# One of a unit's sixteen turns of maxima folded in the loop: a relu by ScalarE and one pass of VectorE in place of two reductions

## The chip, the cores and the metric

The kernel runs on one core of a Trainium2 chip. The metric is the device time of the whole program in microseconds, taken as the median of several executions. The profiled execution is one more of them, seen from inside.

## What is computed

The input is x, 2 sequences of 1024 tokens of 128 features. The reference is one layer of a transformer with the norm behind each part: sixteen-head attention with heads of 8 features, a residual and a layer norm, then a feed-forward part with weights that are small whole numbers, a residual and a second norm.

```python
scores = einsum('bhqd,bhkd->bhqk', q, k) * (1 / sqrt(16))
attn = softmax(scores, axis=-1)
out = einsum('bhqk,bhkd->bhqd', attn, v)
x = layernorm(x + out @ wo.T + bo)
h = silu(x @ w1.T * s1) * (x @ w2.T * s2)
h = gelu(h @ h1.T * s); h = gelu(h @ h2.T * s)
x = layernorm(x + h @ w3.T * s3)
```

The change touches only the maximum of each row of scores, which the softmax subtracts.

## The kernel before, in words

**Units.** Attention is done in 16 units (U_ALL). A unit is one of two sequences, a group of four heads (HG) of the sixteen, and one half of the queries (512, C). Units 2g and 2g+1 share group g of keys and queries, which lie in slot g % 2 of the tiles kx and qx. The scores are computed twice. The first time they have queries on the partitions and keys along a row, only to find each row's largest score. The second time they have keys on the partitions, so that their exponentials can be fed to the products with v. The maxima enter this second pass as additional rows of qx, which is why they have to be there before a unit's first score tile.

**Turns and halves.** A unit has 16 turns (TURNS): four heads by four blocks of 128 queries. Turn t has two halves, m = 2t and 2t+1, one for each 512 of the 1024 keys. For each half TensorE does one matmul of 128x512 into one of four PSUM banks (turn_half, L1265), and VectorE takes its largest value by a TENSOR_REDUCE (turn_half of VectorE, L976). TensorE waits before half m until the reduction of half m-4 has emptied the bank. When a unit's 16 turns are done, larger (L986) takes the smaller of the two negated maxima. POOL then splits them into three bfloat16 parts (split_max, L828 to L834), TensorE turns them (L1314), ScalarE copies them out (copy_max, L671), and SP sends them by two DMAs into qx (load_max, L405). The score tile that begins a unit waits for these DMAs (mrow_in).

**The folded turns of the prologue.** Turns 5 to 26 are done in another way, because ScalarE is free there. With d = k1 - k0, the difference of the two key halves of one head, max(q.k0, q.k1) = q.k0 + relu(q.d). TensorE computes q.d and q.k0 (fold_apart, fold_first), ScalarE takes the relu of q.d out of PSUM into SBUF (copy_over, L684), and VectorE adds q.k0 and takes the maximum in one pass (turn_folded, L966). That pass is two instructions in the profile: the custom operation and the read of its accumulator. The difference of keys is made for group 0 only, from proj, split in two parts, sent through d_dram, and loaded as kd.

**The loop.** From turn 27 (WHOLE) on, halves, scores and products are interleaved by groups g, written out in the program: three halves (turn_halves), three score tiles (scores_of, L1327) in pairs with them, and then 384 columns of products of each of four heads (product, L1343). Maxima are 54 halves ahead of the scores: half m stands beside score tile m - 54. A score tile needs a PSUM bank of three (bank_plan). Its bank comes free when ScalarE has taken the exponential of an earlier tile (exp, L663), as a rule that of three tiles before. At the end of a unit ScalarE copies the unit's products out (copy_unit, L676), and the bank plan moves the score tiles to the bank that this empties. After turn 255 the rest of the units goes on without maxima. VectorE's and SP's parts are hardware loops over four units (Fori, ITERS); those of TensorE and ScalarE are written out.

**SP's queue.** Before its loop SP issues, in the order of the program: unit 0's maxima, loads of group 1, stores of batch 1's keys and queries to DRAM, the biases and wo, five small vectors, and it waits for the stores. Then the loop begins with the maxima of unit 1.

Of the kernel before, what the change touches and what calls it, by code (L numbers as in the profile page):

```python
# [36 lines left out]
H, DH = 16, 8  # L37
# [30 lines left out]
FOLD = 5  # L68
TURN_AFTER, COPY_AFTER = 5, 6
# [133 lines left out]

def apart_bank(t):
    return FOLD_BANKS[(t - FOLD) % len(FOLD_BANKS)]

# [5 lines left out]
def build(nc, xT, wqT, wkT, wvT, woT, bq, bk, bv, bo, late,  # L212
          w1s, w2s, h1s, h2s, w3s, k_dram, q_dram, d_dram, den_dram, out):
    with ExitStack() as ctx:
# [17 lines left out]
        kd_part = [w_high[:, PAIR + j, :] for j in range(HALVES)]  # L232
        w_low = nc.alloc_sbuf_tensor_at("w_low", [P, SLICES, HID], F32, offset=LATE_AT)
# [18 lines left out]
        def over_sb(t):  # L252
            return attn[:, U_ALL - 4 + t % 4, :]

# [64 lines left out]
        kd_in = sem("kd_in")  # L319
        over = sem("over")  # L320
# [92 lines left out]
        def _(sp):  # L413
# [50 lines left out]

            def load_max(i, w):

                sp.wait_ge(max_copied, i * PER + w + 1)
                for r in range(2):
                    spread_max(sp, r, w)
# [13 lines left out]
            for r in range(2):  # L483
                for i in range(HALVES):
                    at = r * GROUP + i * HALVES * DH
                    sp.dma_start(kd[at:at + HALVES * DH].bitcast(F32),
                                 d_dram[r * PAIR:(r + 1) * PAIR].rearrange("h d j t -> (d j) h t"))\
                      .then_inc(kd_in, 16)
# [15 lines left out]
            load_q(1, 1, 1)  # L504
            sp.wait_ge(split_late, 2)
# [16 lines left out]

            with sp.Fori(0, ITERS - 1) as i:
# [4 lines left out]
                for slot in range(2):  # L528
                    base, g = i * (STEPS * HG) + slot * 2 * KT * HG, i * 2 + slot + 2
                    sp.wait_ge(scores, base + KT * HG)  # L530
                    load_q(g, slot, 0)
                    sp.wait_ge(scores, base + KT * HG * 3 // 2)
                    load_k(g, slot, 0, C, rows_in[slot][0])
                    load_max(i, 2 * slot + 2)
                    sp.wait_ge(scores, base + KT * HG * 2)
                    load_k(g, slot, C, L, rows_late[slot])
                    load_q(g, slot, 1)
                    if slot == 0:
                        load_max(i, 3)
# [68 lines left out]
        def _(act):  # L608
# [38 lines left out]
            act.dma_start(d_dram[:, :, 0].rearrange("h d t -> (h d) t"), kd_part[0][0:HG * DH, :])\  # L647
               .then_inc(apart_out, 16)
            act.wait_ge(apart_low, 1)
            act.dma_start(d_dram[:, :, 1].rearrange("h d t -> (h d) t"), kd_part[1][0:HG * DH, :])\  # L650
# [34 lines left out]

            for t in range(FOLD, WHOLE):
                copy_over(t)
                if t == TURNS + COPY_AFTER:
                    copy_max(0)
            for g in range(-RUN_BEFORE, GROUPS_ALL):  # L690
# [4 lines left out]
                else:  # L695
                    late_unit = None
                for n in scores_of(g):
                    exp(n)
# [83 lines left out]
        def _(pool):  # L782
# [67 lines left out]
            split_max(None, 0)  # L850
            pool.wait_ge(v_ready, NC_)
# [63 lines left out]
        def _(dve):  # L915
# [55 lines left out]
            def turn_half(i, m):  # L971

                dve.wait_ge(max_scores, i * (2 * PER * TURNS) + m + 1)
                t = m // 2
                h, q = head_of(t % (PER * TURNS) + PER * TURNS)
                nc.vector.tensor_reduce(negmax[:, t // TURNS % 2, m % 2, h * QT + q:h * QT + q + 1],  # L976
# [225 lines left out]
        def _(pe):  # L1202
# [41 lines left out]
            def turn_half(m):  # L1244
# [4 lines left out]
                if 2 * WHOLE <= m < 2 * WHOLE + 4:  # L1249

                    pe.wait_ge(max_taken, 2 * (m - WHOLE - 3))
                elif m >= 4:

                    pe.wait_ge(max_taken, m - 3)
# [3 lines left out]
                if part == 0:  # L1258
# [3 lines left out]
                    elif t % TURNS == 0:  # L1262

                        pe.wait_ge(rows_in[slot][qc], (t // (PER * TURNS) + 1) * LOAD_INC[qc])
                nc.tensor.matmul(ps[:, half_bank(m), :],  # L1265
                                       qx[at, slot, qc, h, q * P:(q + 1) * P],
                                       kx[at, slot, h, part * C:(part + 1) * C], start=True, stop=True)\
# [337 lines left out]
```

## Time and profile before

| | us |
|---|---|
| median of 3 runs | 445.57 (444.91 to 445.75) |
| the profiled execution's own time | 443.76 |
| its span, first to last instruction | 442.0 |
| TensorE busy | 427.3 |
| VectorE busy | 386.2 |
| ScalarE busy | 367.7 |
| POOL busy | 90.4 |

PE is TensorE's matmuls, PEld its loads of weights, DVE is VectorE, ACT ScalarE, and SPq the issue of DMAs by SP. A row of the groups by line has the line, the engine, the operation, out<-in by the program's names, partitions x elements and the count; then the busy time in us and the mean ns of one; then the idle time of the engine ahead of them, and what ended it. Where instructions overlap at their ends, busy time divided by count is the time from one to the next. A row of the timeline has the start in us, the length in us, the engine, the line, the operation and the count, and in brackets the idle time of the engine before it and who ended that. In the chain a row is start, length and what ran.

### The profile page before, as it was taken

How to read it: one execution, taken by the hardware profiler on the slowest of the kernel's cores; microseconds unless marked ns; L12 is line 12 of the kernel's file. 1: busy time of each engine (PE TensorE's matmuls, PEld its weight loads, DVE VectorE, ACT ScalarE, POOL GpSimd, SP SyncE). 2: the span in 40 equal slices, each digit the busy share in tenths (PEclk: the TensorE clock that was granted, in tenths of full speed). 3: DMA queues.
4: the chain of work that ended last, by engine and by line, in shares of the span. 5: the costliest groups of instructions: out<-in, count | busy, mean ns of one | idle time of the engine just before them, and what ended most of it. 6: DMA issues, size and time to landing. Idle time of an engine off the chain costs nothing.

```text
span 442.0 us, 9804 instructions
## 1 busy us (share of the span) xinstructions
PE 427.3 (97%) x3484; PEld 226.0 (51%) x3484; DVE 386.2 (87%) x721; ACT 367.7 (83%) x694; POOL 90.4 (20%) x142
## 2 busy tenths in 40 slices
PE   8999999999999999999999999999899899999993
PEld 3544444444444444444444443544333488877882
DVE  6699999999999999999999999999874576657636
ACT  4487989988998999989899899999899885678762
POOL 9820000100000010000001002372311363046103
PEclk9998999999999999999999999999999999999998
DMA  5566741100130111013011011121021000000101
GB/s 157 170 208 135 264 146 33 45 27 28 47 122 25 46 31 28 27 47 122 25 50 29 26 27 49 15 42 53 12 43 44 13 8 1 1 2 2 47 1 47
DMA packets 17117, 24.88 MB, mean 56 GB/s; under 512 B 5169, under 2 KB 9009, under 8 KB 16689
## 3 DMA queue, kind: packets, MB, share of 16 engines
q1 hardware_dynamic: 16464, 23.68, 19.0%
q10 hardware_dynamic: 608, 0.59, 0.5%
q8 instruction: 30, 0.49, 0.5%
q14 instruction: 15, 0.11, 0.1%
HBM read 15.08 MB, written 7.60 MB: 51 GB/s over the span
## 4 chain that ended last, share of the span: by engine, by line
PE 81%; DVE 10%; ACT 5%; issue 2%; DMA 0%; POOL 0%; SPq 0%; POOLq 0%; DVEq 0%; ACTq 0%
PE ps L1343 26%; PE ps L1265 20%; PE ps L1450 15%; PE ps L1327 11%; DVE negmax L976 9%; ACT arena L663 2%; PE ps L1206 2%; PE ps L1217 2%; PE ps L1396 1%; PE ps L1293 1%; PE ps L1237 1%; ACT v_pad L721 1%; PE ps L1281 1%; DMA qx<-mT 0%; PE ps L1406 0%
## 5 line engine op out<-in xcount | busy, mean ns | idle before, releaser
L976 DVE TENSOR_REDUCE negmax<-ps 128x1 f32<-128x512 f32 x458 | 275.5, 677 | 1.1 <-PE ps L1265 1.0
L663 ACT ACTIVATE arena<-ps 128x512 f32<-128x512 f32 x360 | 190.1, 605 | 18.5 <-PE ps L1327 13.6
L1327 PE MATMUL ps<-qx,kx 64*128 64x512 f32 x512 | 171.0, 453 | 1.3 <-DVE negmax L976 0.9
L1265 PE MATMUL ps<-kx,qx 61*128 61x512 f32 x468 | 160.6, 442 | 0.7 <-ACT arena L684 0.6
L1265 PEld LDWEIGHTS ps<-kx,qx 61*128 61x128 f32 x468 | 75.5, 185 | 89.2 <-DVE negmax L976 79.3
L1343 PE MATMUL ps<-arena,v_pad 128*32 128x256 f32 (+3 forms) x1328 | 105.2, 408 | 2.9 <-ACT arena L663 2.9
L663 ACT ACTIVATE hf<-ps 128x512 f32<-128x512 f32 x152 | 83.1, 603 | 9.3 <-PE ps L1327 8.3
L1327 PEld LDWEIGHTS ps<-qx,kx 64*128 64x128 f32 x512 | 79.2, 185 | 18.0 <-ACT arena L663 11.0
L1450 PE MATMUL ps<-hid,w_high 128*128 128x512 f32 (+1 forms) x296 | 68.2, 387 | 0.8 <-issue 0.4
L1450 PEld LDWEIGHTS ps<-hid,w_high 128*128 128x128 f32 x296 | 54.2, 188 | 12.3 <-issue 0.8
L1343 PEld LDWEIGHTS ps<-arena,v_pad 128*32 128x32 f32 x1328 | 28.6, 108 | 37.2 <-issue 31.1
L1343 PE MATMUL ps<-hf,v_pad 128*32 128x128 f32 (+1 forms) x600 | 47.5, 388 | 0.0
L1107 DVE TENSOR_TENSOR hid<-hf,hid 128x512 fp32r<-128x512 f32 x32 | 23.0, 726 | 19.6 <-ACT hid L737 19.6
L828 POOL TENSOR_TENSOR mpart<-negmin,zeros 128x16 bf16<-128x16 f32 x15 | 3.3, 221 | 144.4 <-DVE negmin L986 144.4
L887 POOL TENSOR_TENSOR hid<-hf,hid 128x512 fp32r<-128x512 f32 x16 | 20.6, 1320 | 32.6 <-ACT hid L727 32.6
L1343 PEld LDWEIGHTS ps<-hf,v_pad 128*32 128x32 f32 x600 | 15.7, 109 | 16.1 <-issue 9.8
L808 POOL COPY v_pad<-v_sb 128x256 f32 (+1 forms) x8 | 3.1, 398 | 87.2 <-PE ps L1343 87.1
L736 ACT ACTIVATE hf<-ps,h2s_sb 128x512 f32<-128x512 f32 x16 | 11.0, 687 | 10.7 <-PE ps L1450 10.7
L736 ACT ACTIVATE hf<-ps,h1s_sb 128x512 f32<-128x512 f32 x16 | 11.0, 686 | 8.7 <-PE ps L1450 8.7
L1089 DVE SCALAR_TENSOR_TENSOR hf<-ps,w2s_sb,v_pad 128x512 f32<-128x512 f32 x16 | 11.5, 740 | 7.3 <-ACT v_pad L721 7.3
L856 POOL TENSOR_TENSOR w_low<-late_sb,w_high 128x512 fp32r<-128x512 f32 x11 | 14.1, 1282 | 16.4 <-ACT w_high L710 16.4
L1450 PE MATMUL ps<-prt,w_high 128*128 128x512 f32 x64 | 16.4, 403 | 0.6 <-DVE hf L1089 0.6
(98 smaller groups left out, 313.4 us busy)
## 6 DMA issues: line engine op xcount, KB each, us to landing
qx<-parts_q SPq DMA_DIRECT2D x60, 64.0 KB, 2.1
late_sb<-in_late SPq DMA_DIRECT2D x3, 1280.0 KB, 5.6
kx<-parts_k SPq DMA_DIRECT2D x56, 64.0 KB, 2.1
parts_q<-prt SPq DMA_DIRECT2D x3, 512.0 KB, 5.2
parts_q<-arena SPq DMA_DIRECT2D x3, 512.0 KB, 6.8
xT_sb<-in_xT SPq DMA_DIRECT2D x4, 256.0 KB, 4.2
xT_sb<-arena SPq DMA_DIRECT2D x28, 32.0 KB
prt<-den SPq DMA_DIRECT2D x7, 128.0 KB
```

The source lines that it names most:

```text
L663: nc.scalar.activation(probs(n // HG)[:, heads(n), :], ps[:, PLAN["score", n][0], :], ACT.Exp, scale=SCALE).then_inc(exp_done, 1)
L736: nc.scalar.activation(hf[:, m % RING, :], bank, ACT.Gelu, scale=scale).then_inc(gelu_done, 1)
L856: nc.gpsimd.tensor_tensor(half(w_low[:, n, :]), w_sb[:, n, :], w_high[:, n, :], ALU.subtract).then_inc(w_left, 1)
L887: nc.gpsimd.tensor_tensor(half(dst[:, 1, m, :]), hf[:, m % RING, :], dst[:, 0, m, :], ALU.subtract).then_inc(gate_ready, 1)
L976: nc.vector.tensor_reduce(negmax[:, t // TURNS % 2, m % 2, h * QT + q:h * QT + q + 1], ps[:, MAX_BANK + m % 4, :], AX.X, ALU.max, negate=T ...
L1089: return nc.vector.scalar_tensor_tensor(out=out, in0=ps[:, gate_bank(c, m) + 1, :], scalar=s_sb["w2s"][:, m:m + 1], in1=gate[:, m % 2, :], ...
L1107: nc.vector.tensor_tensor(half(dst[:, 1, m, :]), hf[:, m % RING, :], dst[:, 0, m, :], ALU.subtract).then_inc(gelu_ready, 1)
L1206: nc.tensor.matmul(ps[:, bank, 0:cols], nonzero[:, 0, 0:P], nonzero[:, 0, 0:cols], start=True, stop=True)
L1265: nc.tensor.matmul(ps[:, half_bank(m), :], qx[at, slot, qc, h, q * P:(q + 1) * P], kx[at, slot, h, part * C:(part + 1) * C], start=True, s ...
L1327: nc.tensor.matmul(ps[:, bank, :], kx[at, slot, h % PAIR, kt * P:(kt + 1) * P], qx[at, slot, qc, h % PAIR, :], start=True, stop=True)\
L1343: ins = nc.tensor.matmul(ps[32 * n:32 * n + 32, PLAN["pv", w][0], c0:c1], v_pad[:, w // QC % 2, kt, n, :], probs(k)[:, n, c0:c1], start=(k ...
L1450: return nc.tensor.matmul(dsts[n], half(stationary), half(moving), start=start, stop=stop)
```

## The change

In the loop, one turn of each unit is folded too: turn t with t % 16 = 12, from 28 to 236, which is 14 turns. For it

- TensorE computes q.d in the place of half 2t and q.k0 in the place of half 2t+1. The half that uses the bank of q.d next waits for the relu (over) and not for a reduction.
- ScalarE does the relu of q.d (copy_over_one) ahead of the exp of the score tile that stands beside half 2t.
- VectorE skips half 2t, and at half 2t+1 does one pass of the kind of turn_folded.

The differences of keys are needed for one head of each group (FOLD_HEAD). Those of batch 0 come from kd_part of the prologue. Those of batch 1 are made by POOL in three more passes over 128x512. SP stores both to d_dram and loads each group's head into kd_one: for group 1 ahead of the loop, for the others within it. Two stores for batch 0 stand before those of batch 1's keys. Two for batch 1, a wait for the landing of all four, and the load for group 1 stand right before the loop.

```diff
 FOLD = 5
+FOLD_AT, FOLD_END, FOLD_HEAD = 12, 240, 1
 TURN_AFTER, COPY_AFTER = 5, 6
...
+def folded(t):
+    return t % TURNS == FOLD_AT and WHOLE <= t < FOLD_END
+def folds_to(t):
+    return WHOLE - FOLD + (t - FOLD_AT) // TURNS
 def apart_bank(t):
...
         kd_part = [w_high[:, PAIR + j, :] for j in range(HALVES)]
+        kd_late = [w_high[:, PAIR + 3 + j, :] for j in range(HALVES)]
+        kd_one = w_high[:, PAIR + 5:PAIR + 7, :].bitcast(F32R)
         w_low = nc.alloc_sbuf_tensor_at("w_low", [P, SLICES, HID], F32, offset=LATE_AT)
...
             return attn[:, U_ALL - 4 + t % 4, :]
+        kd_both = attn[:, 3, :]
+        def over_one(t):
+            return attn[:, U_ALL - 2 + t // TURNS % 2, :]
...
         kd_in = sem("kd_in")
+        late_apart = sem("late_apart")
+        late_apart_out = sem("late_apart_out")
+        one_in = [sem(f"one_in{n}") for n in range(2)]
         over = sem("over")
...
+            def store_apart(b, g0, parts):
+                for j in range(HALVES):
+                    sp.dma_start(d_dram[b * NG + g0:(b + 1) * NG, :, :, j].rearrange("g h d t -> (g h d) t"),
+                                 parts[j][g0 * HG * DH:, :]).then_inc(late_apart_out, 16)
+            def load_one(g, slot):
+                for i in range(HALVES):
+                    sp.dma_start(kd_one[i * HALVES * DH:(i + 1) * HALVES * DH, slot, :].bitcast(F32),
+                                 d_dram[bass.ds(g, 1), FOLD_HEAD].rearrange("o d j t -> (o d j) t"))\
+                      .then_inc(one_in[slot], 16)
             def load_max(i, w):
...
                     sp.dma_start(kd[at:at + HALVES * DH].bitcast(F32),
-                                 d_dram[r * PAIR:(r + 1) * PAIR].rearrange("h d j t -> (d j) h t"))\
+                                 d_dram[0, r * PAIR:(r + 1) * PAIR].rearrange("h d j t -> (d j) h t"))\
                       .then_inc(kd_in, 16)
...
             load_q(1, 1, 1)
+            store_apart(0, 1, kd_part)
             sp.wait_ge(split_late, 2)
...
+            sp.wait_ge(late_apart, 3)
+            store_apart(1, 0, kd_late)
+            sp.wait_ge(late_apart_out, 2 * STORE_INC)
+            load_one(1, 1)
             with sp.Fori(0, ITERS - 1) as i:
...
                     load_q(g, slot, 0)
+                    load_one(g, slot)
                     sp.wait_ge(scores, base + KT * HG * 3 // 2)
...
             act.wait_ge(apart_high, 1)
-            act.dma_start(d_dram[:, :, 0].rearrange("h d t -> (h d) t"), kd_part[0][0:HG * DH, :])\
+            act.dma_start(d_dram[0, :, :, 0].rearrange("h d t -> (h d) t"), kd_part[0][0:HG * DH, :])\
                .then_inc(apart_out, 16)
             act.wait_ge(apart_low, 1)
-            act.dma_start(d_dram[:, :, 1].rearrange("h d t -> (h d) t"), kd_part[1][0:HG * DH, :])\
+            act.dma_start(d_dram[0, :, :, 1].rearrange("h d t -> (h d) t"), kd_part[1][0:HG * DH, :])\
                .then_inc(apart_out, 16)
...
                 nc.scalar.activation(over_sb(t), ps[:, apart_bank(t), :], ACT.Relu).then_inc(over, 1)
+            def copy_over_one(t):
+                act.wait_ge(max_scores, 2 * t + 1)
+                act.wait_ge(max_taken, 2 * (t - 4))
+                nc.scalar.activation(over_one(t), ps[:, half_bank(2 * t), :], ACT.Relu).then_inc(over, 1)
...
                     late_unit = None
+                ones_at = [m for m in turn_halves(g) if folded(m // 2) and m % 2 == 0]
                 for n in scores_of(g):
+                    if ones_at and n == scores_of(g)[ones_at[0] - turn_halves(g)[0]]:
+                        copy_over_one(ones_at[0] // 2)
                     exp(n)
...
             split_max(None, 0)
+            pool.wait_ge(max_split, 1)
+            for r in range(2):
+                nc.gpsimd.memset(kd_one[ROWS:GROUP, r].bitcast(F32), 0.0).then_inc(kd_set, 1)
+                pool.wait_ge(kd_set, r + 3)
+            pool.wait_ge(max_taken, 2 * WHOLE)
+            nc.gpsimd.tensor_tensor(kd_both, proj[:, 1, :], proj[:, 0, :], ALU.subtract).then_inc(late_apart, 1)
+            pool.wait_ge(late_apart, 1)
+            nc.gpsimd.tensor_copy(kd_late[0].bitcast(F32R), kd_both).then_inc(late_apart, 1)
+            pool.wait_ge(late_apart, 2)
+            nc.gpsimd.tensor_tensor(kd_late[1].bitcast(F32R), kd_both, kd_late[0], ALU.subtract).then_inc(late_apart, 1)
+            pool.wait_ge(late_apart, 3)
             pool.wait_ge(v_ready, NC_)
...
-                dve.wait_ge(max_scores, i * (2 * PER * TURNS) + m + 1)
                 t = m // 2
                 h, q = head_of(t % (PER * TURNS) + PER * TURNS)
+                one = folded(t) and not (isinstance(i, int) and not folded(i * PER * TURNS + t))
+                if one and m % 2 == 0:
+                    return
+                dve.wait_ge(max_scores, i * (2 * PER * TURNS) + m + 1)
+                if one:
+                    dve.wait_ge(over, i * PER + folds_to(t))
+                    nc.vector.tensor_tensor_reduce(over_one(t), ps[:, MAX_BANK + m % 4, :], over_one(t),
+                                                   -1.0, 3.0e38, ALU.add, ALU.min,
+                                                   negmax[:, t // TURNS % 2, 0, h * QT + q:h * QT + q + 1])\
+                      .then_inc(max_taken, 2)
+                    return
                 nc.vector.tensor_reduce(negmax[:, t // TURNS % 2, m % 2, h * QT + q:h * QT + q + 1],
...
                     pe.wait_ge(max_taken, 2 * (m - WHOLE - 3))
+                elif folded((m - 4) // 2) and m % 2 == 0:
+                    pe.wait_ge(over, folds_to((m - 4) // 2))
                 elif m >= 4:
...
                         pe.wait_ge(rows_in[slot][qc], (t // (PER * TURNS) + 1) * LOAD_INC[qc])
+                keys = kx[at, slot, h, part * C:(part + 1) * C]
+                if folded(t):
+                    g = t // (QC * TURNS)
+                    if part == 1:
+                        keys = kx[at, slot, h, 0:C]
+                    elif g == 0:
+                        keys = kd[at, h, :]
+                    else:
+                        pe.wait_ge(one_in[slot], (g + 1) // 2 * STORE_INC)
+                        pe.wait_ge(kd_set, 4)
+                        keys = kd_one[at, slot, :]
                 nc.tensor.matmul(ps[:, half_bank(m), :],
                                        qx[at, slot, qc, h, q * P:(q + 1) * P],
-                                       kx[at, slot, h, part * C:(part + 1) * C], start=True, stop=True)\
+                                       keys, start=True, stop=True)\
                   .then_inc(max_scores, 1)
...
     q_dram = nc.dram_tensor("parts_q", (HALVES, QC, G_ALL, HG, DH, HALVES, C), F32, kind="Internal").ap()
-    d_dram = nc.dram_tensor("parts_d", (HG, DH, HALVES, C), F32, kind="Internal").ap()
+    d_dram = nc.dram_tensor("parts_d", (G_ALL, HG, DH, HALVES, C), F32, kind="Internal").ap()
     den_dram = nc.dram_tensor("den", (B, HG, NG, L), F32, kind="Internal").ap()
```

## Rows read from the trace of the kernel before

**Rows 1.** The page's first part: busy time and share of the span.
```profile
PE 427.3 (97%) x3484; PEld 226.0 (51%) x3484; DVE 386.2 (87%) x721; ACT 367.7 (83%) x694; POOL 90.4 (20%) x142
```

**Rows 2.** Groups by line, VectorE: busy us, mean ns, idle us before them.
```profile
L976 DVE TENSOR_REDUCE negmax<-ps 128x1 f32<-128x512 f32 x458 | 275.5, 677 | 1.1 <-PE ps L1265 1.0
...
L966 DVE CUSTOM_DVE_ANT_0 arena<-ps,arena 128x512 f32<-128x512 f32 x22 | 13.5, 687 | 0.2 <-ACT arena L684 0.2
...
L966 DVE DVE_READ_ACCUMULATOR2_ANT negmax<- 128x1 f32 x22 | 1.8, 84 | 0.0
```

**Rows 3.** The chain of waits in time order (start, us), 170 to 200.
```profile
175.48 0.79 PE ps L1343 x16
...
177.59 0.78 PE ps L1343 x8
...
179.28 0.78 PE ps L1343 x8
...
191.71 0.78 PE ps L1343 x8
...
193.50 0.78 PE ps L1343 x8
```

**Rows 4.** Timeline at a unit's boundary, 171.5 to 181.
```profile
173.24 1.58 ACT L663 ACTIVATE hf<-ps 128x512 f32<-128x512 f32 x3 [0.29 <-PE ps L1327]
...
174.98 0.50 PE L1327 MATMUL ps<-qx,kx 64*128 64x512 f32 x1
...
176.42 0.62 ACT L676 ACTIVATE arena<-ps 128x512 f32<-128x512 f32 x1
...
178.30 0.49 PE L1265 MATMUL ps<-kx,qx 61*128 61x512 f32 x1
...
179.62 0.16 DVE L986 TENSOR_TENSOR negmin<-negmax 128x16 f32<-128x16 f32 x1
```

**Rows 5.** Timeline at another unit's boundary, 150 to 162.
```profile
157.85 0.85 PE L1343 MATMUL ps<-arena,v_pad 128*32 128x384 f32 x8 [0.40 <-ACT arena L663]
```

**Rows 6.** Timeline of SP, 20 to 75.
```profile
52.03 0.43 SPq L518 DMA_DIRECT2D h1s_sb<-in_h1s  x1
52.50 0.43 SPq L518 DMA_DIRECT2D h2s_sb<-in_h2s  x1
53.24 1.59 SPq L405 DMA_DIRECT2D qx<-mT  x2
```

**Rows 7.** Timeline of ScalarE, 48 to 49.5.
```profile
48.54 0.30 ACT L671 ACTIVATE mT<-ps 128x128 f32<-128x128 bf16 x1
```

**Rows 8.** Timeline of all engines, 53 to 63.
```profile
52.72 10.89 DVE L976 TENSOR_REDUCE negmax<-ps 128x1 f32<-128x512 f32 x18
...
56.39 0.18 PEld L1327 LDWEIGHTS ps<-qx,kx 64*128 64x128 f32 x1 [0.36 <-issue]
```

**Rows 9.** DMA issues by line: size and median us from issue to landing.
```profile
parts_k<-arena SPq DMA_DIRECT2D x1, 512.0 KB, 4.4
parts_k<-prt SPq DMA_DIRECT2D x1, 384.0 KB, 3.2
...
parts_k<-prt SPq DMA_DIRECT2D x1, 128.0 KB, 2.0
```

**Rows 10.** Groups by line, POOL.
```profile
L845 POOL TENSOR_TENSOR arena<-late_sb,prt 128x512 f32<-128x512 f32 x4 | 5.0, 1268 | 1.2 <-ACT prt L657 1.2
```

**Rows 11.** Busy time by stretch (PE, PEld, DVE, ACT, POOL), granted clock, DMA.
```profile
39.50:41.00 1.50, 1.50 (x7) 1.28 (x6) 1.50 (x3) 1.50 (x5) 0.00 (x0) 0.50 1.00 127
41.00:43.00 2.00, 2.00 (x12) 0.62 (x10) 2.00 (x4) 1.56 (x4) 0.00 (x0) 0.53 1.12 195
43.00:45.00 2.00, 2.00 (x28) 1.06 (x26) 1.37 (x5) 1.31 (x3) 0.00 (x0) 1.00 1.02 362
```

**Rows 12.** Timeline of TensorE, 31 to 44.
```profile
40.25 1.05 PE L1265 MATMUL ps<-kx,qx 61*128 61x512 f32 x2
...
43.12 0.49 PE L1265 MATMUL ps<-kx,qx 61*128 61x512 f32 x1
```

## The prediction

> **What bounds the kernel now.** I first read the page's busy shares: TensorE 97%, VectorE 87%, ScalarE 83% [rows 1]. They make TensorE look like the bound. The groups by line say otherwise: 458 maxima of a half (L976) cost 275.5 us of VectorE, so 0.60 us each back to back, and the engine idled only 1.1 us before all of them [rows 2]. From about 37 to 315 us VectorE never rests. The chain of waits then gives TensorE's pace. A group of the order (three key halves for maxima, three score tiles, 384 columns of products) starts every 1.79 us when VectorE sets it (3 x 0.60), and every 1.69 us right after a delay, when TensorE is catching up: 177.59 to 179.28. Once per unit, where ScalarE copies the unit out, a group takes 2.11 us: 175.48 to 177.59 [rows 3]. So TensorE's own time is close behind. Per unit (32 halves, 10.67 groups) VectorE needs 32 x 0.60 = 19.2 us. TensorE alone needs 10.67 x 1.69 = 18.0, plus 0.42 at that boundary, plus some 0.2 to 0.3 for the turn of the maxima: 18.7.
>
> **What a folded turn saves.** Turns 28, 44, ... 236 are folded: 14. Each loses two reductions, 1.20 us, and gets one pass as in the prologue: 13.5 / 22 = 0.61 us, its accumulator read of 0.08 beside the next pass (0.70 if it isn't) [rows 2]. VectorE is asked for 0.59 us less each, 8.3 us in all. The two matmuls stay. ScalarE gets a relu of 0.60 us, 0.49 in a row of others (three exps take 1.58, so 0.49 from start to start) [rows 2, 4].
>
> **What is kept of it.** I walk one fold through the rows. In the group at 173 us it falls on the second and third pair, so the relu stands between the exps of 173.24 and 173.73. The third exp then starts at 174.69 and not at 174.21, and ends at 175.29. The score tiles have three PSUM banks, so the third tile of the next group, now at 174.98, waits for that exp: 175.34, 0.36 later. ScalarE reaches the copy-out of the unit at 176.7, not 176.42, and the third tile after it waits for the copied bank, so the group of 178.30 starts near 178.6 [rows 4]. Its first half can be reduced from 179.13. Before, VectorE took it at 179.02, 0.60 ahead of the step that starts at 179.62 [rows 4]. So VectorE's 0.59 us is gone 1.6 groups after the fold, with 0.1 us on top; it has simply waited for TensorE. Behind that its queue refills at 1.79 - 1.69 = 0.1 us a group, which is enough until the next fold. The fold moves by one place in the group of three from unit to unit. The same walk with the relu first in its group gives a gain of 0.08 (boundary 0.18 later). With the relu third it gives a loss of 0.20: there the next unit's products wait for an exp behind the copy, as at 157.85 [rows 5], and VectorE had no lead left. Twelve folds from turn 60 on, four of each kind: 0.32 - 0.40 - 0.80 = -0.9; turn 44 like the middle kind, -0.1; turn 28 lies ahead of the wait below, 0. **Folds: 1.0 us slower.** Bounds: a relu wholly on the path, 13 x 0.49 = 6.4 us slower. On the other side, without the push by ScalarE, a boundary yields VectorE's lead of about 0.2 and 0.1 of catching up: 13 x 0.3 = 3.9 us gained; with no limit but VectorE, 8.3.
>
> **What is moved: SP's queue.** This is the large term. SP issues DMAs without a pause before its loop, 0.47 us apart (52.03, 52.50), and only at 53.24 does it issue the two DMAs that bring unit 1's maxima (L405) [rows 6]. ScalarE had copied those maxima out of PSUM at 48.54 [rows 7], so SP alone is late. TensorE waits for them: the first score tile of unit 1 loads its weights only at 56.39 after 0.36 us idle, and all later work of TensorE stands behind it. VectorE works on without a gap, but only just [rows 8]. The change puts ahead of that point: store_apart of batch 0, 2 DMAs, 0.94 us; store_apart of batch 1, 0.47 to its second issue; the wait for its landing; load_one, 2 DMAs, 0.94. The landing of a 256 KB store has no row: 128 KB took 2.0 us, 384 KB 3.2 [rows 9]. I take 2.9, nearer to the larger, since two go together, and keep 2.0 and 4.4 as ends. Sum 0.94 + 0.47 + 2.9 + 0.94 = **5.25 us** (4.35 to 6.75). Nothing hides it. The POOL steps that feed batch 1's store (three of 1.27 us, as [rows 10], behind the prologue's last pass at about 37.6) end near 42, so that wait is no term. In the loop load_one adds 0.94 us to SP per group of heads, between waits for tile 32 and tile 48 of a unit pair, nine us apart: nothing. POOL's other additions (two small memsets) end before unit 1's maxima are there: nothing.
>
> The Trainium skill, page "DMA: Bandwidth & Descriptors", section "Anatomy of one DMA", gives some 2.0 us fixed plus bytes over 436 GB/s; for 256 KB that is an estimate of 2.6 us, and the sum would be 0.3 less. The 384 KB row lies above its 2.9.
>
> **The clock after the wait.** The granted clock fell to 1.2 GHz at 39.5 us, after much smaller gaps of TensorE, [rows 11]. A group then took 2.87 us (40.25 to 43.12) [rows 12] against 1.69, and the next one was fast again, so it stayed low for some 3.4 us. A stop of over 5 us should bring this again. Behind the stop VectorE has no lead, so each slow group costs 1.2 us in full. With some 3.4 us of it, as in the rows, that is 1.2 groups: **1.4 us** (0 to 2.2).
>
> The Trainium skill, page "TensorE: Matmul & The Clock Gate", Part 1, reckons half of the time at the lower clock as lost; for the same 3.4 us that is an estimate of 1.7 us.
>
> **Sum.** The profiled execution took 443.76 us: + 5.25 + 1.4 + 1.0 = 451.4, 7.65 more. It is 1.8 under the median of the runs, 445.57, so the median should be 445.57 + 7.65 = 453.2 us.
>
> **Rivals.**
> (a) Part of the gain is kept. If ScalarE's idle fifth of a microsecond per group [rows 4] takes up the relu, each of 13 folds gives 0.3: 445.57 + 6.65 - 3.9 = 448.3. Against it: the three score banks.
> (b) All is kept, the other side: VectorE's demand alone sets the time, and TensorE follows at less than 1.69 us per group, since its pieces overlap more once no bank is awaited. Then 8.3 us against 6.65: 443.9, faster by 1.7. It decides once more than 0.5 us of each 0.59 is kept. For it: VectorE's unbroken work. Against it: all groups that catch up show 1.69, none less.
> (c) SP's wait doesn't decide, because the maxima come in time after all: only the folds count, 446.6. Against it: TensorE waits for them already.
> (d) The relu stands wholly on the path: 445.57 + 6.65 + 6.4 = 458.6. Against it: ScalarE idles about 0.2 us in most groups.
> That the change doesn't do what it says I see no way for: 28 reductions go, 14 passes come.
>
> **How the numbers follow.** Forecast 0.72, its own range 451.0 to 456.0 (stop 4.35 to 6.75, clock 0 to 2.2, folds 0 to 2.5, not all at one end); (a) 0.13, (b) 0.04, (c) 0.03, (d) 0.08. The range 448.0 to 457.0 takes in (a) and leaves out (b), (c) and (d). A measurement of this kernel tells 0.2% (0.9 us) from no change. Faster by more: (b), 0.04, and a fortunate (a), 0.01. Within: 0.03, of (c). Slower: the rest, 0.92.
>
> **What would show it.** In the changed kernel: SP's L405 pair before the loop near 58.5 instead of 53.24; TensorE and VectorE both idle for about 5 us from 56 to 61.7; the granted clock at 1.2 GHz for some us behind it; VectorE no longer without idle time, with some 0.4 to 0.6 us of waiting near each unit boundary; the pace of a unit still 19.2 us; score tiles that wait for ScalarE one group behind a relu. I am wrong if unit 1's maxima are issued at 53 us, or if units shrink to 18.7 us.

## The result, and the profile after

| | before | after |
|---|---|---|
| median, 4 runs each on the same chip | 445.66 (444.91 to 446.0) | 453.15 (451.69 to 453.43) |
| the profiled execution's own time | 443.76 | 453.24 |
| its span | 442.0 | 451.5 |

The ratio is 1.0176, 95% interval 1.0156 to 1.0196: **slower by 1.8%**, 7.5 us. The page of the kernel after, its busy shares and three of its groups (the first answers to L976, the third to L1327):

```profile
PE 431.6 (96%) x3484; PEld 233.1 (52%) x3484; DVE 381.6 (85%) x721; ACT 373.2 (83%) x708; POOL 94.6 (21%) x147
...
L1044 DVE TENSOR_REDUCE negmax<-ps 128x1 f32<-128x512 f32 x430 | 261.9, 684 | 11.1 <-PE ps L1348 10.1
...
L1410 PE MATMUL ps<-qx,kx 64*128 64x512 f32 x512 | 172.1, 452 | 6.5 <-DMA qx<-mT 5.1
```

The change did what it says: 28 reductions fewer (430 against 458), and VectorE is busy 4.6 us less in all [rows 1]. Its idle time ahead of the reductions went from 1.1 us [rows 2] to 11.1. TensorE waits 5.1 us for the maxima's DMA (qx<-mT). The 14 new passes, in the groups by line of VectorE:

```profile
L1039 DVE CUSTOM_DVE_ANT_0 arena<-ps,arena 128x512 f32<-128x512 f32 x14 | 9.7, 691 | 3.5 <-PE ps L1348 2.0 <-ACT arena L728 0.6
```

They last 691 ns against 687 in the prologue, as expected. The timeline of SP shows where the stop comes from (L551 are the small vectors, L487 store_apart, L493 load_one, L424 unit 1's maxima):

```profile
53.95 0.43 SPq L551 DMA_DIRECT2D h1s_sb<-in_h1s  x1
54.42 0.43 SPq L551 DMA_DIRECT2D h2s_sb<-in_h2s  x1
55.16 0.82 SPq L487 DMA_DIRECT2D parts_d<-w_high  x2
57.88 0.81 SPq L493 DMA_DIRECT2D w_high<-parts_d  x2
59.33 1.61 SPq L424 DMA_DIRECT2D qx<-mT  x2
```

The maxima are issued at 59.33 and not at 53.24 [rows 6]. This execution began 0.70 us later than that of before (by the first folded pass of the prologue, 24.80 against 24.10), so 5.39 us belong to the queue (59.33 - 53.24 - 0.70). TensorE and VectorE behind it, in the timeline of all engines:

```profile
57.30 0.50 PE L1348 MATMUL ps<-kx,qx 61*128 61x512 f32 x1
...
62.48 0.76 PE L1410 MATMUL ps<-qx,kx 64*128 64x512 f32 x1 [4.68 <-DMA qx<-mT]
...
65.44 0.69 DVE L1044 TENSOR_REDUCE negmax<-ps 128x1 f32<-128x512 f32 x1 [5.80 <-PE ps L1348]
```

And the same stretch as busy time by window (the stretch and its length; TensorE's matmuls, weights, VectorE, ScalarE, POOL; then the granted clock, 1.00 for 2.4 GHz and 0.50 for 1.2; last the DMA engines' share and GB/s):

```profile
58.00:60.00 2.00, 0.00 (x0) 0.00 (x0) 1.64 (x3) 0.37 (x1) 0.00 (x0) 1.00 0.13 37
60.00:62.00 2.00, 0.00 (x0) 0.00 (x0) 0.00 (x0) 0.00 (x0) 0.00 (x0) 0.91 0.04 12
62.00:64.00 2.00, 1.52 (x9) 0.48 (x9) 0.00 (x0) 0.60 (x1) 0.00 (x0) 0.50 0.90 241
64.00:66.00 2.00, 2.00 (x14) 0.83 (x6) 0.56 (x1) 0.53 (x2) 0.00 (x0) 0.50 0.99 417
66.00:68.00 2.00, 2.00 (x20) 0.98 (x20) 0.83 (x3) 1.53 (x4) 0.00 (x0) 0.50 0.60 170
68.00:70.00 2.00, 2.00 (x24) 1.16 (x23) 1.55 (x3) 1.52 (x4) 0.00 (x0) 0.89 0.00 0
```

TensorE stands for 4.7 us, and when it has work again it has it at 1.2 GHz until about 68.4.

**How the rest is read.** Each unit ends its maxima with one `larger` (L986 before, L1054 after), 15 in all. I took their starts in both traces, counted from the first folded pass of the prologue (which takes the start of the program out), and the difference after minus before from one to the next. That gives the shift that each unit adds, in us. The first entry holds all up to the end of unit 1's maxima (turn 28 among it). The second holds turn 44 and the stop. From the third on there is one fold in each up to turn 236 (the last but one).

| kernel | up to unit 1 | unit 2 | units 3 to 15 | sum |
|---|---|---|---|---|
| after | 0.76 | 7.18 | -0.22 0.33 0.05, -0.22 0.32 0.04, -0.22 0.34 0.05, -0.22 0.62 -0.11, 0.16 | 8.87 |
| queue_alone | 0.16 | 7.42 | all 0.00, but one 0.02 | 7.59 |
| after_filled | 0.98 | 5.62 | as after | 7.49 |
| before_delay5 | 0.13 | 3.83 | 0.00 | 3.96 |
| before_early_max | 0.71 | 0.13 | 0.00 to 0.03 | 0.86 |
| early_nofold | -0.04 | -0.04 | -0.02 to 0.07 | -0.06 |
| before_again | 0.15 | 0.58 | 0.00 to 0.01 | 0.75 |
| after_early_max | 0.98 | 0.48 | as after | 2.36 |
| early_end_210 | 0.61 | -0.20 | as after up to turn 204, then 0.15 0.01 0.00 | 0.81 |
| early_short | 0.03 | -0.22 | -0.42 0.11 -0.18, three times to 0.02, then -0.42 0.27 -0.53, 0.16 | -2.19 |
| early_relu_last | 0.91 | 0.62 | 1.15 0.14 0.63, three times, then 1.15 0.34 -0.02 0.06 | 8.82 |
| fold_at_4 | 0.70 | 1.14 | 0.16 0.14 0.06, ... | 3.64 |
| fold_at_0 | -1.02 | 1.13 | 0.19 -0.06 0.29, ... | 2.30 |

The steps of the folds from turn 60 on repeat to 0.02 us from cycle to cycle, so in units 3 to 15 this view shows far smaller differences than the runs' times do. The first two entries don't repeat so well: the same kernel (before_again) has 0.15 and 0.58 there, and each row is one execution.

For what stands behind the stop there is a measure within one execution: from the start of unit 1's first score tile to the next `larger`. By the timelines it is 7.89 us in before (56.42 to 64.31), 7.91 in before_again, 9.40 in before_delay5 (59.00 to 68.40), 10.33 in queue_alone (61.81 to 72.14), 10.47 in after (62.48 to 72.95) and 8.20 in after_filled (62.58 to 70.78). In after and after_filled turn 44 is folded in it.

### The profile page after: what moved, and what is told of

The parts are those of the page before. It is cut to its first block, busy times and chain, and to the rows that moved or that the text cites. A ratio compares the mean times of both kernels' runs of the same rounds, so it can differ in the third digit from the quotient of the medians.

```text
span 451.5 us, 9903 instructions
## 1 busy us (share of the span) xinstructions
PE 431.6 (96%) x3484; PEld 233.1 (52%) x3484; DVE 381.6 (85%) x721; ACT 373.2 (83%) x708; POOL 94.6 (21%) x147
## 4 chain that ended last, share of the span: by engine, by line
PE 78%; ACT 7%; DVE 6%; SPq 3%; issue 3%; DMA 3%; POOL 0%; POOLq 0%; DVEq 0%; ACTq 0%
PE ps L1426 25%; PE ps L1348 19%; PE ps L1533 15%; PE ps L1410 10%; DVE negmax L1044 5%; ACT arena L701 3%; PE ps L1274 2%; PE ps L1285 2%; DMA parts_q<-arena 2%; PE ps L1479 1%; PE ps L1376 1%; SPq L453 1%; PE ps L1305 1%; SPq L481 1%; ACT v_pad L768 1%
## 5 line engine op out<-in xcount | busy, mean ns | idle before, releaser
L1044 DVE TENSOR_REDUCE negmax<-ps 128x1 f32<-128x512 f32 x430 | 261.9, 684 | 11.1 <-PE ps L1348 10.1
L1348 PE MATMUL ps<-kx,qx 61*128 61x512 f32 x454 | 154.4, 436 | 0.6 <-ACT arena L722 0.6
L1348 PEld LDWEIGHTS ps<-kx,qx 61*128 61x128 f32 x454 | 74.2, 187 | 76.3 <-DVE negmax L1044 59.0
L1426 PE MATMUL ps<-arena,v_pad 128*32 128x256 f32 (+3 forms) x1328 | 106.4, 413 | 2.9 <-ACT arena L701 2.9
L1410 PEld LDWEIGHTS ps<-qx,kx 64*128 64x128 f32 x512 | 80.5, 186 | 28.6 <-ACT arena L701 12.8
```

What stands on the lines that cost most here:

```text
L1348: nc.tensor.matmul(ps[:, half_bank(m), :], qx[at, slot, qc, h, q * P:(q + 1) * P], keys, start=True, stop=True)\
L1410: nc.tensor.matmul(ps[:, bank, :], kx[at, slot, h % PAIR, kt * P:(kt + 1) * P], qx[at, slot, qc, h % PAIR, :], start=True, stop=True)\
L1426: ins = nc.tensor.matmul(ps[32 * n:32 * n + 32, PLAN["pv", w][0], c0:c1], v_pad[:, w // QC % 2, kt, n, :], probs(k)[:, n, c0:c1], start=(k ...
```

## The experiments

Labels with `early` hold the same edit: unit 1's maxima are sent before the biases, and the loop sends the next ones at its end. So in the diffs.

### The queue without the folds: queue_alone

```diff
 def folded(t):
-    return t % TURNS == FOLD_AT and WHOLE <= t < FOLD_END
+    return False
```

> No turn is folded in the loop; the stores, the wait for their landing, the loads and POOL's steps of the change stay, so the maxima are those of the kernel before. Theory Q (SP's queue delays unit 1's maxima, then the lower clock): 5.4 us of queue and 1.4 to 2.5 us of clock over the kernel before, so 445.7 + 7 = 452 to 454, nearly all that the change costs. Rival F (the folded turns cost it, by ScalarE): no more than 446.5, since nothing is folded. If it is 450 to 451, the lower clock costs nothing.

451.91 us against 444.58 on the same chip, ratio 1.0163 (1.0132 to 1.0194). So 7.3 of the 7.5 us come without a single fold. In the timeline of SP the maxima's DMAs stand at:

```profile
58.62 1.61 SPq L424 DMA_DIRECT2D qx<-mT  x2
```

This execution began 0.25 later than the first of before, so the queue gives 58.62 - 0.25 - 53.24 = 5.13 us. The shift is 7.59; the 2.5 us above the queue need another cause.

### The stores kept, the maxima sent first: after_early_max, before_early_max, early_nofold

```diff
             store_q(...)
+            load_max(0, 1)
+            sp.wait_ge(late_apart_out, STORE_INC)
+            load_one(1, 1)
             sp.dma_start(bo_bc[:], bo.partition_broadcast(P)).then_inc(in_mid, 16)
...
             sp.wait_ge(late_apart_out, 2 * STORE_INC)
-            load_one(1, 1)
             with sp.Fori(0, ITERS - 1) as i:
-                load_max(i, 1)
...
-                    if slot == 0:
-                        load_max(i, 3)
+                    load_max(i, 3 if slot == 0 else PER + 1)
...
-            load_max(ITERS - 1, 1)
```

> The changed kernel with SP's order mended: unit 1's maxima go out right behind the stores of queries, the load for group 1 waits only for the two stores of batch 0, and the last wait stands before the loop where nothing is urgent. Theory Q with neutral folds: the stop is gone, what is left is turn 28 (0.8 us in the profile after), a unit cycle of three folds that gives -0.22 + 0.33 + 0.05, and the last folds (0.7), less the 0.4 to 0.6 us that TensorE waits for unit 1's maxima in the kernel before too: 446 to 447.5. Rival B (the folds gain 0.59 us each once the stop no longer hides it): 438 to 440. Rival D (the relu is on the path): 450 or more.

> The kernel before with unit 1's maxima sent before the biases, wo and the small vectors; nothing else. Theory Q: TensorE waits 0.36 to 0.6 us for them in the kernel before and VectorE had no lead behind it, so 0.0 to 0.5 us faster: 445.2 to 445.7. If the queue were not on the path at all, 445.7. It also is what after_early_max must be compared with.

> SP's mended order of after_early_max with all its stores, loads and POOL's steps, and no turn folded in the loop. Theory Q: once unit 1's maxima go out early, the rest of the moved work costs nothing: equal to the kernel before and to before_early_max, 1.0 to 2.0 us under after_early_max; the difference to after_early_max is the price of the folded turns alone, which the traces put at 1.5 us. Rival: the added DMAs or POOL's passes cost something by themselves (by traffic in the stretch 36 to 50 us), 446 or more.

after_early_max took 446.2 against 444.58 (1.0036, 1.0021 to 1.0051), before_early_max 445.17 against 444.58 (1.001, 0.9993 to 1.0026), early_nofold 445.3 against 444.85 (ratio 0.9991, 0.9971 to 1.0012, so no difference shown). With unit 1's maxima out of the way of the new DMAs, 6 of the 7.5 us are gone: **the order of SP's queue was the loss, not the DMAs and not POOL's passes** (early_nofold has all of them, at no cost that the runs show). The maxima sent early bring the kernel before no gain that the runs show, where 0 to 0.5 us were expected. Whether TensorE's 0.36 us there were covered stays open: the profile of before_early_max also had a longer low stretch of the clock near 40 us (last section). What is left, 1.0 to 1.6 us by the medians and 2.36 - 0.86 = 1.5 by the shifts, is the folds. With the whole relu the folds gained in no run.

### The clock behind the stop: after_filled, before_delay5

```diff
+                if n == KT * HG:
+                    for _ in range(6):
+                        nc.tensor.matmul(ps[:, bank, :], xT_sb[:, 0:P], xT_sb[:, 0:C], start=True, stop=True)
                 if n % (KT * HG) == 0:
```

> The changed kernel; TensorE runs six matmuls of f32, 512 columns each (some 0.85 us each, 5.1 us in all), into the free bank of unit 1's first score tile before it waits for the maxima, so that it doesn't idle in the stop. Output unchanged. Theory Q with the clock: the granted clock stays at 2.4 GHz behind the stop, which saves 1.5 to 2.5 us: 450.7 to 451.6. Rival (the lower clock is hidden behind VectorE or ScalarE): 453.1 as the changed kernel. If the six matmuls outlast the stop, up to 0.5 us are lost again.

In before_delay5 five DMAs of h2s into a spare tile stand before the loop of the kernel before.

> The kernel before with five more small DMAs (2 KB each, into a tile that nothing reads) in SP's queue ahead of its loop, 0.47 us each, so 2.35 us. Nothing else. Theory Q: unit 1's maxima come 2.35 us later and VectorE has no lead, so 2.35 us slower, 0.47 per DMA; if the stop is too short for the clock to fall, 2.3 to 2.6 in all, with a fall of the clock 3.5 to 5. Rival (the queue isn't on the path): 0.

The windows of after_filled show the stop with TensorE at work in it, and a clock that doesn't fall:

```profile
60.00:62.00 2.00, 2.00 (x6) 0.86 (x5) 0.00 (x0) 0.00 (x0) 0.00 (x0) 1.00 0.51 92
62.00:64.00 2.00, 2.00 (x13) 0.55 (x13) 0.00 (x0) 0.60 (x1) 0.00 (x0) 1.00 0.88 358
64.00:66.00 2.00, 2.00 (x26) 0.97 (x24) 1.11 (x2) 1.64 (x4) 0.00 (x0) 1.00 0.98 344
```

Its shift is 7.49 against 8.87, so 1.4 us less, though the filling matmuls ended some 0.9 us after the maxima had landed. Together the low clock costs about 2.3 us of after's time. The measure within one execution says the same: 10.47 - 8.20 = 2.3 between after and after_filled, and 10.33 - 7.89 = 2.4 for queue_alone. So do the shifts: 7.59 - 5.13 = 2.5 in queue_alone, and 8.87 - 5.39 - 1.0 (the folds, below) = 2.5 in after. The medians don't show it: after_filled took 451.79 against 444.58 (1.0165, 1.0129 to 1.0201), 7.2 us more, where after is 7.5 over its own before; 450.7 to 451.6 had been expected. In before_delay5 (447.5 against 444.98, 1.0058, 1.0034 to 1.0081) the stop was shorter, and so was the low stretch:

```profile
60.00:62.00 2.00, 2.00 (x18) 1.07 (x18) 1.11 (x2) 1.18 (x4) 0.00 (x0) 0.58 1.01 425
62.00:64.00 2.00, 2.00 (x22) 0.98 (x14) 0.87 (x3) 0.56 (x3) 0.00 (x0) 0.56 0.70 226
64.00:66.00 2.00, 2.00 (x25) 0.87 (x21) 2.00 (x4) 2.00 (x5) 0.00 (x0) 1.00 0.00 0
```

Its maxima were issued at 55.80, 2.42 later than before's with 0.14 of later start taken off, and the shift is 3.96: 1.5 us for the clock, and 9.40 - 7.89 = 1.5 by the measure within one execution. Here the clock was at 1.2 GHz for 3.4 us; in after and queue_alone it was for 6.8. The medians again show less: 2.5 us in all (1.5 to 3.6), which is hardly more than the queue alone. SP's queue in the kernel before varies (before_again, below), so the median of before needn't have the queue of its first profile; how much that makes is open.

### The fold itself: early_short, early_relu_last

```diff
-                nc.scalar.activation(over_one(t), ps[:, half_bank(2 * t), :], ACT.Relu).then_inc(over, 1)
+                nc.scalar.activation(over_one(t)[:, 0:16], ps[:, half_bank(2 * t), 0:16], ACT.Relu).then_inc(over, 1)
```

> As after_early_max, but ScalarE's relu of a folded turn of the loop covers 16 of the 512 columns; the rest of its tile is stale, so these turns' maxima leave out the true second key half. Everything else, with VectorE's pass, is as it was. Theory S (ScalarE's push through the three score banks eats VectorE's 0.59 us): the relu's 0.49 falls to about 0.2, and a cycle of three folds goes from +0.15 to about -0.6, so 3 us under after_early_max (about 443 where before is 444.6). Rival T (TensorE's own pace at the boundary eats it, whatever ScalarE does): within 1 us of after_early_max.

441.69 against 444.98, 0.9921 (0.99 to 0.9941). The relu of 16 columns takes 184 ns:

```profile
L727 ACT ACTIVATE arena<-ps x14: 178/184/225, 39.0 to 287.9; 128x16 f32<-128x16 f32 x14
```

Three folds then give 0.42 - 0.11 + 0.18 = 0.49 us where with the whole relu they cost 0.15. So the length of the relu takes 0.64 us of three folds, 0.2 of each. But even nearly without it only 0.5 of the 3 x 0.59 = 1.8 us of VectorE come out. That TensorE's own time keeps the other 1.3 is the likely reason and is argued, not shown. For it: VectorE's idle time ahead of its reductions is 3.1 us in early_short, 2.7 of it ended by TensorE, against 1.1 in before [rows 2]. So both theories hold in part: the relu's length costs, and most of VectorE's gain stays away even without it. In the other run the relu stands behind the last exp of the group.

```diff
                 for n in scores_of(g):
-                    if ones_at and n == scores_of(g)[ones_at[0] - turn_halves(g)[0]]:
-                        copy_over_one(ones_at[0] // 2)
                     exp(n)
+                    if ones_at and n == scores_of(g)[-1]:
+                        copy_over_one(ones_at[0] // 2)
```

> As after_early_max, but ScalarE does the relu of a folded turn behind the last exp of its group of three and not ahead of the exp beside it. Theory S: the exps of this group are no longer pushed, so the third score tile of the next group isn't late by the relu; but VectorE waits for the relu 1.0 to 1.6 us where the pair is early in its group and has only 0.59 us to give, and the half four places on waits for the relu too: a cycle of three folds at +0.5 to +2, so 448 to 453. Rival (the relu's place is free as long as its sum on ScalarE is the same): as after_early_max, 446.

453.97 against 444.85, 1.0193 (1.0164 to 1.0222). Three folds cost 1.15 + 0.14 + 0.63 = 1.9 us instead of 0.15. The pass's row tells why (groups by line, VectorE):

```profile
L1038 DVE CUSTOM_DVE_ANT_0 arena<-ps,arena 128x512 f32<-128x512 f32 x14 | 9.7, 692 | 15.1 <-ACT arena L727 14.4 <-PE ps L1347 0.7
```

VectorE waits 14.4 us for the relus, 1.0 each, against 0.6 in all in after. Of the two places, ahead of the exp is the better one.

### Another turn of the unit: fold_at_4, fold_at_0

Both are after_early_max with FOLD_AT (and FOLD_HEAD) changed, and SP's two stores of batch 0's differences and the load for group 1 earlier; 13 turns are folded. The diff shows fold_at_4; fold_at_0 has 0, 240, 0.

```diff
-FOLD_AT, FOLD_END, FOLD_HEAD = 12, 240, 1
+FOLD_AT, FOLD_END, FOLD_HEAD = 4, 240, 0
```

> As after_early_max, but the folded turn is t % 16 = 4 (head 0), so the relu stands beside score tile 18 of a unit and not beside 2, ten groups from the next boundary and four behind the last; SP's two stores and the load for group 1 stand still earlier, where SP waited. 13 turns. Theory S: the push comes where VectorE still has little lead and TensorE is catching up, so each push counts 0.2 to 0.36, but VectorE's 0.59 then carries to the boundary: net 0 to 0.3 faster per unit, 442 to 446. Rival T (TensorE's floor of 18.7 to 18.8 us per unit binds with the relu on top): 19.0 to 19.2 per unit, 444 to 446. If the unit comes to 19.27 as with turn 12, the place doesn't matter.

> The same with t % 16 = 0, the relu beside score tile 10, right behind the copy-out of the unit, where ScalarE has caught up. Theory S: as fold_at_4, but VectorE's lead is at its smallest, so TensorE binds for the whole unit: 18.8 to 19.1 per unit, 442 to 445. Rival: the copy and the relu together push the score tiles by 0.3 us and it comes out like turn 12, 446.

447.0 (1.0049, 1.0031 to 1.0067) and 446.44 (1.0044, 1.0025 to 1.0063) against 444.98. A cycle of three costs 0.36 and 0.41 by the shifts, turn 12's costs 0.15. The medians don't tell the three places apart (after_early_max 1.0036, 1.0021 to 1.0051). No place tried gains, and by the shifts 12 was the best of them. Other places were not tried.

### The last folds and the kernel before again: early_end_210, before_again

```diff
-FOLD_AT, FOLD_END, FOLD_HEAD = 12, 240, 1
+FOLD_AT, FOLD_END, FOLD_HEAD = 12, 210, 1
```

> after_early_max without its last two folds (turns 220 and 236), so twelve folds less two; the maxima of these two turns are found by two reductions each as in the kernel before. Theory (the last folds cost more because ScalarE also rounds weights beside them): against the trace of the kernel before, the step of the unit with turn 220 falls from +0.62 us to about 0, that of turn 236 from -0.11 to about 0, and the one behind from +0.16 to about 0; about 0.7 us less in all than with all fourteen. Rival (the weight rounding only shows itself because something else of the change delays it): the steps stay.

> The kernel before, unchanged, profiled a second time. Theory (executions differ by how long and how often the granted clock is low, not by anything in the code): the groups of three halves between 65 and 310 us keep their pace to 0.05 us per unit against the first profile, and any difference of the end of more than 0.5 us goes with a low stretch of the clock that the first profile doesn't have, near 40 us or behind 310 us; such a stretch behind 310 us costs about 1.3 us (as the other profiles with one there suggest). Rival: the executions differ in launch or in DMA landings, and the spread of the end stands at the first instructions.

Both are one execution each. Without turns 220 and 236 the last three steps are 0.15, 0.01, 0.00 and not 0.62, -0.11, 0.16 (with all folds 0.64, -0.12, 0.16 in after_early_max): 0.5 us less, of 0.7 expected. The 0.15 is a delay that the fold of turn 204 leaves. So the last two folds do cost more than their kind. That ScalarE's rounding of weights beside them is the reason fits the place, but no run took the rounding away; it is argued, not shown.

before_again took 444.70 where the first profile took 443.76. Its units from 3 on differ by 0.01 us at most, as expected. Of the 0.94 us, 0.17 stand ahead of the first folded pass, 0.75 between it and unit 3, none behind. The clock doesn't tell them apart: in both it was low for 3.4 us near 40 us and not near 320. SP's queue does. In before_again the maxima were issued at 54.11, which is 54.11 - 53.24 - 0.17 = 0.70 us later than in the first profile. Its timeline of SP, and SP's waits from 40 to 62 us (before has none there):

```profile
52.30 0.43 SPq L518 DMA_DIRECT2D h2s_sb<-in_h2s  x1
54.11 1.59 SPq L405 DMA_DIRECT2D qx<-mT  x2
```

```profile
SPq L521 <- DMA parts_q<-arena: 1.1, 1, 1.1
```

SP waited 1.1 us for a store of batch 1's queries to land. So the rival holds here, by a DMA's landing and the launch, and the theory doesn't. It also shows from the other side that every delay of unit 1's maxima reaches the end: 0.70 us of queue made 0.73 at unit 2's `larger`.

## Why the prediction was right, and where it was not

The forecast was 453.2 us and 7.65 more; the medians show 453.15 and 7.5. Step by step it is less even.

**The bound.** Right. VectorE set the pace with TensorE just behind: with folds VectorE's idle time goes from nearly none to several us, and the end doesn't come earlier. The window of queue_alone from 80 to 300 us, in the same columns:

```profile
80.00:300.00 220.00, 217.81 (x2203) 101.05 (x2205) 219.62 (x378) 200.21 (x394) 21.40 (x56) 1.00 0.15 44
```

And the same window of after:

```profile
80.00:300.00 220.00, 217.73 (x2201) 105.89 (x2193) 215.25 (x376) 203.74 (x403) 19.62 (x56) 1.00 0.16 44
```

TensorE does the same work in the same time; VectorE has 0.4 us to spare in the first and 4.7 in the second. Rivals (a) and (b), a kept gain, are out: of the cycles of three, only those with the relu cut to 16 columns gain.

**SP's queue, 5.25 us.** Right, 5.39 in after and 5.13 in queue_alone. Its parts were off and evened out. Two DMAs for batch 0 moved the last small vector from 52.50 [rows 6] to 54.42, less 0.70: 1.22 us, not 0.94. From the first store of batch 1 to load_one are 2.72 us (55.16 to 57.88), not 0.47 + 2.9 = 3.37: the landing took 2.25 us behind the second issue. From load_one to the maxima are 1.45 (57.88 to 59.33), not 0.94; what SP does in the 0.5 us between isn't in the trace. Rival (c) is out: TensorE waited for the maxima. The Trainium skill, page "DMA: Bandwidth & Descriptors", section "Anatomy of one DMA", has a fit for DMAs that GpSimd issues; it made the landing an estimate of 2.6 us. The trace says 2.25 for these, which SP issues: nearer to it than to my 2.9.

**The clock, 1.4 us.** The mechanism was right, the size wrong. This is **the step that failed**: "With some 3.4 us of it, as in the rows". The rows of before [rows 11] showed the clock low for 3.4 us after small gaps; behind a stop of 4.7 us it was low for 6.8, and it cost 2.3 to 2.5 us. before_delay5 had the 3.4 us and cost 1.5, which is what the term was made for. The upper end of 2.2 was too low too. The Trainium skill, page "TensorE: Matmul & The Clock Gate", Part 1, counts half of the time at the lower clock as lost. For before_delay5 that is an estimate of 1.7 us (1.5 shown), for after, with TensorE at work from 62.48 to about 68.4, of 3.0 (2.3 to 2.5 shown): above both. That part of the low stretch had nothing to delay would explain it and isn't shown.

**The folds, 1.0 us.** Right: 8.87 - 7.59 = 1.28 between after and queue_alone, of which 5.39 - 5.13 = 0.26 is SP's queue, so 1.0. The twelve from turn 60 on sum to 0.92 in the table, and 0.9 was predicted. The kinds were ordered rightly and each came out larger or smaller: relu first a gain of 0.22 (0.08), third a loss of 0.33 (0.20), second a loss of 0.05 (0.10), so a cycle costs 0.15 and not 0.22. The last two folds with what they leave cost about 0.5 for themselves, for which I had no term; that made up for it, which was luck. Turns 28 and 44 were put at 0 and 0.1. Against queue_alone they come to 0.60 - 0.24 = 0.36 in after, less the same 0.26: 0.1, or 10.47 - 10.33 = 0.14 by the measure within one execution. The walk itself can be seen at the fold of the third kind, in the timeline:

```profile
163.06 0.61 ACT L728 ACTIVATE arena<-ps 128x512 f32<-128x512 f32 x1
...
163.54 2.09 ACT L701 ACTIVATE arena<-ps 128x512 f32<-128x512 f32 x4
...
166.79 0.85 PE L1426 MATMUL ps<-arena,v_pad 128*32 128x384 f32 x8 [0.41 <-ACT arena L701]
...
168.11 0.69 DVE L1044 TENSOR_REDUCE negmax<-ps 128x1 f32<-128x512 f32 x1 [0.27 <-PE ps L1348]
```

Two exps of the group come before the relu at 163.06 and one behind it. The products of 166.79 wait 0.41 us for an exp behind the copy-out, as [rows 5] foretold, and VectorE, out of its lead, waits 0.27 at 168.11. Rival (d), the relu wholly on the path at 0.49 a fold, is out at 0.1 a fold; early_relu_last shows what it looks like, 0.64 a fold.

**The step from the profiled execution to the median, 1.8 us.** The prediction added the changes to 443.76 and then carried the distance to the median over. That distance didn't carry over: after's profile, 453.24, lies on its median, 453.15. By the profiles the change is 9.48 us: 0.70 of later start, 5.39 queue, 2.5 clock, 1.0 folds, and -0.1 at the end. The prediction missed the profile by 1.8 us (451.4): 0.7 the start, 1.1 the clock, 0.1 the queue, nothing the folds, -0.1 the end. It hit the median by luck, only because the 1.8 us that it carried over, and that after's profile didn't have, stood in for these. The medians themselves differ by 7.5 and not by 9.5 because before's first profile lies low among its executions: 443.76 where the median is 445.66, and before_again took 0.94 us more. Three things were found that vary among executions: SP's wait for a store to land ahead of the maxima (none in before, 1.1 us in before_again, 0.2 in after), the clock near 40 us, low for 3.4 us, for 6.8 (before_early_max) or not at all (early_nofold, fold_at_0), and a second low stretch near 320 us in some. How often each comes in the unprofiled runs stays open, and so does whether the stop at 60 us in after takes something out of their spread.

## What to carry to other kernels

When a change adds DMAs and a wait to a queue, look first at what the next item of that queue is for: here stores, a wait for their landing and a load, placed ahead of the one DMA that TensorE waited for, cost 7.3 us (queue_alone), and with that DMA ahead of them nothing that the runs show (early_nofold). A shorter pass on the busiest engine is worth only the distance to the next engine's own time (here 0.16 us of 0.59 with the relu cut short), and it must be weighed against what the helper engine is pushed by (0.2). Don't carry the distance of one profiled execution to the median over to the changed kernel: profile twice and see which stretches differ.

## What the hardware showed that I had not expected

**A stop has a second price.** TensorE stood 4.7 us and the granted clock was then at 1.2 GHz for 6.8 us, for 2.3 to 2.5 us of time; with the shorter stop of before_delay5 (2.15 us) it was 3.4 us and 1.5. Whether the price follows the length of the stop isn't shown: these are three profiles, and near 40 us both lengths of the low stretch turn up in nearly the same program. Matmuls on data at hand during the stop kept the clock up (1.00 in after_filled).

**The clock falls in some executions and not in others of nearly the same program.** The windows of before_early_max near 40 us, where it stayed low for 6.8 us:

```profile
38.00:40.00 2.00, 2.00 (x9) 1.52 (x7) 2.00 (x4) 2.00 (x5) 0.00 (x0) 0.60 1.01 129
40.00:42.00 2.00, 2.00 (x12) 1.45 (x14) 2.00 (x4) 2.00 (x6) 0.00 (x0) 0.50 1.09 144
42.00:44.00 2.00, 2.00 (x12) 0.74 (x6) 0.91 (x2) 0.46 (x1) 0.00 (x0) 0.50 1.10 180
44.00:46.00 2.00, 2.00 (x22) 0.90 (x22) 1.97 (x4) 1.58 (x3) 0.44 (x2) 0.70 1.01 410
```

And those of early_nofold, at 1.0 there, but with a low stretch at 317.4, where the kernel passes from attention to the rest and TensorE has little to do for a moment:

```profile
39.00:41.00 2.00, 2.00 (x11) 0.89 (x9) 2.00 (x4) 2.00 (x5) 1.86 (x3) 1.00 0.99 124
41.00:43.00 2.00, 2.00 (x14) 0.74 (x13) 2.00 (x4) 2.00 (x5) 0.74 (x1) 1.00 1.12 148
315.00:317.00 2.00, 0.73 (x5) 0.30 (x5) 0.73 (x3) 0.87 (x2) 0.94 (x5) 1.00 0.00 0
317.00:319.00 2.00, 2.00 (x11) 0.46 (x13) 2.00 (x2) 1.47 (x4) 1.17 (x1) 0.61 0.01 4
319.00:321.00 2.00, 2.00 (x10) 0.99 (x14) 2.00 (x2) 1.38 (x3) 0.00 (x0) 0.53 0.08 18
```

From the last `larger` to the end of the span all profiled executions take 127.0 us (126.90 to 127.02), but the three with a low stretch near 320 us (early_nofold, early_relu_last, fold_at_4) take 128.3: that stretch costs 1.3 us, and it is there or not from one execution to another. Such things, with SP's wait of up to 1.1 us above, are of the size of the spread of some 2 us among runs of this kernel; that they make it up isn't shown, as the unprofiled runs have no trace.
